# One core, graph network on Trainium2: in the message stage, both subtractions of the bfloat16 split on VectorE, and four of seven bins scaled by ScalarE

## The reference

```
for l in range(N_LAYERS):                      # 3
    f1 = relu(x[row] @ nb_W[l] + nb_b[l]);  f2 = relu(x[col] @ self_W[l] + self_b[l])
    h = relu(concatenate([f1, f2], axis=1) @ att1_W[l] + att1_b[l])
    mask = clip(sigmoid(h @ att2_W[l] + att2_b[l]) * (ZETA - GAMMA) + GAMMA, 0.0, 1.0)
    rowsum = segment_sum(mask, row, num_segments=n) + 1e-06
    d_inv_sqrt = clip(rowsum ** (-0.5), 0.0, 10.0)
    vals = mask * d_inv_sqrt[row] * d_inv_sqrt[col]
    x = segment_sum(vals[:, None] * x[col], row, num_segments=n)
    out = out + x
```

## Time and profile before

| | before |
|---|---|
| median of 3 runs | 4532.59 us (4524.75 to 4538.07) |
| the profiled execution | 4528.35 us, of which the span from first to last instruction is 4526.7 us |
| message stage, first layer | from the first scaling at 1960.68 us to the last `take` at 2422.54 us |
| message stages of all three layers | about 3 x 462 us, three tenths of the span |
| TensorE matmul, VectorE, GpSimd, ScalarE busy over the whole span | 87%, 82%, 56%, 43% |

### The profile page before, as it was taken

One profiled execution on the slowest core, in us unless ns is written; L12 is line 12 of the kernel. 1 busy time (PEld: TensorE's weight loads), 2 busy tenths in 40 slices (PEclk: granted clock), 3 DMA queues, 4 the chain that ended last, 5 costly groups with the idle time before them and its releaser, 6 DMA issues. The chain is left out here.

```text
span 4526.7 us, 258560 instructions
## 1 busy us (share of the span) xinstructions
PE 3923.0 (87%) x100368; PEld 3766.8 (83%) x100369; DVE 3699.7 (82%) x5871; ACT 1952.9 (43%) x4743; POOL 2522.8 (56%) x3439
## 2 busy tenths in 40 slices
PE   5888857888875999979997999979998899979997
PEld 5888857777774999968886999978887899979887
DVE  6666678988886888889996788889997788879998
ACT  4666636777762121135553111235554111125554
POOL 4555538978862222268885222248897222238987
PEclk7777769999997999989998999989999999989999
DMA  1000009999992777746662677746663677656665
GB/s 29 1 1 1 1 1 273 315 299 294 285 273 81 236 247 241 240 138 171 171 171 84 229 241 239 247 149 171 171 171 89 207 241 247 236 170 173 171 171 139
DMA packets 532058, 793.93 MB, mean 175 GB/s; under 512 B 66324, under 2 KB 466120, under 8 KB 531976
## 3 DMA queue, kind: packets, MB, share of 16 engines
q1 hardware_dynamic: 499048, 714.07, 49.5%
q0 software_dynamic: 32928, 78.72, 7.6%
HBM read 672.34 MB, written 120.24 MB: 175 GB/s over the span
## 5 line engine op out<-in xcount | busy, mean ns | idle before, releaser
L1330 POOL TENSOR_TENSOR message<-message 128x448 f32<-128x448 f32 x1029 | 1243.5, 1241 | 209.5 <-ACT message L1314 209.4
L1101 PE MATMUL pre_ps<-rows_a,hotT_a 128*128 128x64 bf16 x21609 | 1289.2, 193 | 52.1 <-DMA hotT_a<-hot_scratch 27.3
L1101 PE MATMUL pre_ps<-table,hotT_a 128*128 128x64 bf16 x21609 | 1288.7, 194 | 0.0
L1101 PEld LDWEIGHTS pre_ps<-rows_a,hotT_a 128*128 128x128 fp8e4 x21609 | 1131.3, 98 | 59.0 <-issue 58.8
L1101 PEld LDWEIGHTS pre_ps<-table,hotT_a 128*128 128x128 fp8e4 x21609 | 1131.8, 98 | 1.1 <-issue 1.0
L1341 DVE TENSOR_TENSOR message<-message 128x448 f32<-128x448 f32 x1029 | 994.2, 966 | 69.0 <-POOL message L1330 68.9
L1181 DVE SCALAR_TENSOR_TENSOR weighed<-pre_ps,w 128x448 f32<-128x448 f32 x1029 | 642.4, 624 | 309.5 <-PE pre_ps L1101 217.1
L1314 ACT ACTIVATE message<-high_ps,mask 128x64 f32<-128x64 f32 x3087 | 699.6, 326 | 298.4 <-PE high_ps L1273 279.2
L1285 PE MATMUL sum_ps<-message,hot_b 128*128 128x192 bf16 x7203 | 784.0, 247 | 7.4 <-DVE message L1341 5.7
L1273 PE MATMUL low_ps<-table,hot_b 128*128 128x64 bf16 x12348 | 528.7, 193 | 161.0 <-DMA hot_b<-hot_scratch 64.9
L1149 POOL TENSOR_SCALAR fresh<-gate 128x49 f32<-128x49 f32 x147 | 35.3, 240 | 1113.5 <-ACT gate L1129 1113.5
(11 more groups left out here) (149 smaller groups left out, 5130.0 us busy)
## 6 DMA issues: line engine op xcount, KB each, us to landing
hotT_a<-hot_scratch SPq DMA_DIRECT2D x1029, 224.0 KB, 4.6
hot_b<-hot_scratch SPq DMA_DIRECT2D x1029, 224.0 KB, 2.8
hot_scratch<-hot SPq DMA_DIRECT2D x343, 336.0 KB, 9.3
hot_a<-hot_scratch SPq DMA_DIRECT2D x147, 784.0 KB, 5.1
places<-slots_scratch POOLq DMA_DIRECT2D x686, 112.0 KB, 6.6
out<-res SPq DMA_DIRECT2D x1, 1536.0 KB
slots_scratch<-bins SPq DMA_DIRECT2D x49, 12.5 KB
raw<-in_src SPq DMA_DIRECT2D x1, 768.0 KB
```

Source lines behind the costliest of these rows:

```text
L1101: last = nc.tensor.matmul(pre_ps[g][:, j, :], hotT[:, b, g, end, j * P:(j + 1) * P].bitcast(FP8), table, start=end + part == 0, stop=end = ...
L1330: pool.tensor_tensor(message[:, g, :, 1, :], message[:, g, :, 0, :], top[:, g, :, 0, :, 1], ALU.subtract).then_inc(s["rest_ready"], 1)
```

## The change

LOW goes from 4 to 3: VectorE scales three bins out of PSUM (192 elements) and ScalarE four. The GpSimd block is removed; its subtraction becomes `rest` on VectorE, two groups late, and `third` goes from two groups late to three. VectorE's queue per group is then: scaling(q), rest(q-2), third(q-3), and `take` in the last group. At the end of the stage the left-over differences are written out.

```
-    LOW = min(4, G - 1)
+    LOW = min(3, G - 1)
...
-            @block.gpsimd
-            def _(pool):
-                def row(r, b, nth, first):
-                    for g in range(NG):
-                        q = r * NG + g
-                        pool.wait_ge(s["low_scaled"], q + 4)
-                        pool.wait_ge(s["high_scaled"], q + 4)
-                        pool.tensor_tensor(message[:, g, :, 1, :], message[:, g, :, 0, :], top[:, g, :, 0, :, 1],
-                                           ALU.subtract).then_inc(s["rest_ready"], 1)
-                each_row(pool, NB, row)
-
             @block.vector
             def _(dve):
...
+                def rest(q, r, g, b):
+                    dve.wait_ge(s["low_scaled"], q + 4)
+                    dve.wait_ge(s["high_scaled"], q + 4)
+                    dve.tensor_tensor(message[:, g, :, 1, :], message[:, g, :, 0, :], top[:, g, :, 0, :, 1],
+                                      ALU.subtract).then_inc(s["rest_ready"], 1)
...
-                        late(r, g, b, 2, first, third)
+                        late(r, g, b, 2, first, rest)
+                        late(r, g, b, 3, first, third)
                         if g == NG - 1 and not first:
                             take(r - 1, 1 - b)
                 each_row(dve, NB, row)
+                rest(Q - 2, NB - 1, NG - 2, 0)
+                third(Q - 3, NB - 1, NG - 3, 0)
+                rest(Q - 1, NB - 1, NG - 1, 0)
                 third(Q - 2, NB - 1, NG - 2, 0)
                 third(Q - 1, NB - 1, NG - 1, 0)
                 take(NB - 1, 0)
```

## The result

The changed kernel takes 4575.24 us in the median of four runs (4569.57 to 4582.81), the kernel before, with one more run beside them, 4535.33 us (4524.75 to 4542.38). The forecast was 4563 us, +30.

The account below looks back on a forecast made before the run. A loop through GpSimd and ScalarE was taken to set 9.395 us a row; VectorE's plain sum afterwards gives 9.58. Over 47 rows 8.7 us, plus 0.2 and 1.1 at the ends: 10.0 a layer, +30 for three, 4563 us (4542 to 4602).

Parts of the forecast that it names:

- What bounds the kernel now: Message stage: a row is a loop of GpSimd's seven instructions (8.63 us) plus 0.77 us waiting for ScalarE, 9.40 us.
- already full: VectorE in the message stage: its savings and the 0.53 us paid for each `rest` would nearly cancel.
- Steps 1 to 3: VectorE, message stage: `third` costs 0.53 us instead of 0.94, `rest` 0.53, scaling three bins 0.27 instead of 0.33.
- Steps 4 and 5: Message stage: ScalarE's four-bin scaling has 1.4 us to spare; TensorE's wait for the later `third` stays hidden.
- Step 5: TensorE finishes its gather 1.2 us after `third`, one turn (1.33 us) early; a sum four groups late loses that cover.
- Step 6: VectorE's queue: added semaphore waits of `rest`, 40 to 57 ns each, are worked off beside the running instruction.
- The stage with its ends: Message stage per layer: 8.7 us from 47 rows, +0.2 at the start, +1.1 at the end, together 10.0 us.
- Larger fixed cost: Rival, chance 0.04: VectorE instructions out of PSUM hold it longer; a row grows by 0.48 us, +71 us, near 4633.
- The stretch not GpSimd's: Rival, chance 0.02: both VectorE subtractions keep 0.94 us, 15.3 us a row, +870 us.
- Two subtractions overlapping: Rival, chance 0.05: `third` behind `rest` on VectorE hides the fixed 0.07 us; a row of 9.09 us, near 4494.
- Register work: Rival, chance 0.07: register and wait work in VectorE's queue shows, 0.84 us a row, +123 us, near 4686.

Follow-up runs that it names:

- e4_before_take5: The kernel before, with `take` in the sixth group of a row instead of the seventh: 4456.68 against 4528.82 us, ratio 0.9847.
- e2_pool_low3: The kernel before with LOW = 3 alone, both differences staying where they were: 4529.62 against 4528.82 us, ratio 1.0005.
- e1_low4: The changed kernel with LOW = 4 again, so only the difference is moved to VectorE: 4633.59 us against 4528.82 for the kernel before, ratio 1.0226.
- e7_late4: The changed kernel with LATE = 4 instead of 5 (sum four groups late): 4763.57 us against 4524.94 for the kernel before, ratio 1.0528.
- e3_low2: The changed kernel with LOW = 2, ScalarE scaling five of seven bins: 4495.08 us against 4528.82 for the kernel before, ratio 0.9929.
- e10_low21: The changed kernel with `take` one group earlier and VectorE scaling two bins or one in alternate groups: 4446.89 us against 4506.24 for the kernel before, ratio 0.9875.
- e5_spare_tt: The changed kernel plus an unused GpSimd subtraction of two SBUF tensors per group: 5528.84 us in one run, against 4524.94 for the kernel before.
- e6_spare_memset: The changed kernel plus an unused GpSimd memset of 448 elements per group: 4568.28 us in one run, against 4524.94 for the kernel before.
- e9_after_take5: The changed kernel with `take` in the sixth group of a row instead of the seventh: 4543.28 us against 4506.24 for the kernel before, ratio 1.0088.

## Why the prediction was right, and where it was off

- *What bounds the kernel now.* That a row was a loop through GpSimd with ScalarE's share was right (e4_before_take5). That VectorE was "already full" was wrong: 0.41 us of each stretched `third` were waiting in disguise, absorbing `take` (e4_before_take5) and the shorter scaling (e2_pool_low3) without a trace. The forecast didn't rest on it: it set a plain sum of VectorE's times for the row after beside the measured 9.395 us for the row before. Taken alone, the scaling of three bins was worth nothing in the kernel before; beside the moved difference it gave 0.46 us a row (e1_low4 against the changed kernel).
- *Steps 1 to 3.* The durations were right: 0.53, 0.53 and 0.27 us, and the order of instructions that no row had shown cost nothing more. The row is 9.61 us, not 9.58: the 0.53 is 0.533, fourteen times a row. 0.03 x 141 = 4 us.
- *Steps 4 and 5.* No wait for ScalarE, none for TensorE in the running rows. Step 5's cover was real, and it is gone with a sum four groups late, as the step says. But its 1.2 us for TensorE's part were too low: 1.66 in e7_late4.
- *Step 6.* No gap ahead of `rest` or `third`; the register work is hidden.
- *The stage with its ends.* +10.0 us were forecast for a layer's whole message stage. From the last split of the table before the stage (L1207) to the last `take` the three layers took 480.4 to 480.5 us before and 492.8, 492.8 and 493.9 after: +38 in all, against +30. Beside the 4 us of rounding, the tail is 4.24 us (4.31 in the second layer), not 4.07, and each layer lost 0.6 to 1.7 us in its first two rows. In the first layer TensorE stopped in the midst of a sum:

```profile
1985.38 0.67 PE L1285 MATMUL sum_ps<-message,hot_b 128*128 128x192 bf16 x6 [1.36 <-issue]
```

  and VectorE's next scaling and `rest` came late (10.24 us for that row instead of 9.61). The profile names nothing that TensorE waited for. The kernel before has such stops too, of 1.31 us near the start of its second and third stages, so they aren't the change's own; the cause wasn't tried.
- *The whole.* The two profiled executions differ by 4576.16 - 4528.35 = 47.8 us: 38 in the message stages, 6.5 before the first of them, 3.3 in the two later mask stages, which the change doesn't touch. By the medians it is 40 to 42 us, so of the 12 us above the forecast some 8 are the message stage's (row, ends) and the rest can't be told from differences between runs.
- *The rivals.* Larger fixed cost: refuted, `take` and the scaling at 0.27 and a row that e1_low4, e3_low2 and e10_low21 meet at four sizes of the scaling. The stretch not GpSimd's: refuted by e5_spare_tt and e6_spare_memset. Two subtractions overlapping: refuted, 0.53 and 0.54 in a row. Register work: not seen.

## What to carry to other kernels

When a stretched instruction on one engine goes with another engine's instructions, price the pair and not the single one: here GpSimd's subtraction and VectorE's exclude each other, 0.74 and 0.53 us, but the scaling, a VectorE instruction that reads PSUM, fits into GpSimd's time for nothing. Before moving work off a helper engine, look for what makes it idle: 0.77 and 1.12 us of idle time in alternate rows, behind a `take` that stood one group too late, were worth more than the whole move. And a VectorE that is never idle could be summed from starts to 0.2% here (five kernels, rows of 8.95 to 10.07 us): fill it until it meets the next engine, not to a round share of bins.

## What the runs showed of the hardware that I had not expected

In some runs VectorE's records grow with no change in its pace. In the changed kernel's first message stage a subtraction has a record of 0.61 us at the start and 0.76 at the end, always 0.53 from start to start. In e1_low4 the record goes from 0.62 to 1.18 us; two thirds into the stage it is 1.05:

```profile
2302.24 1.05 DVE L1336 TENSOR_TENSOR message<-message 128x448 f32<-128x448 f32 x1
2302.78 0.85 DVE L1351 TENSOR_TENSOR message<-low_ps,mask 128x256 f32<-128x256 f32 x1
```

Past the first rows VectorE is never idle in either stage, but that alone doesn't do it: in e9_after_take5 and e10_low21 it is never idle either, and the record still stands at 0.63 and 0.61 at the end. In e7_late4, with waits, it stays at 0.61 to 0.62. The end of the record seems to be the real one: the last `take`, which has to wait for the last sum, comes 1.07 us after the end of the last subtraction before and after the change alike, with records of 0.61, 0.76 and (second layer) 0.83. That explains 0.15 us of the longer tail, and the 4.31 us of the second layer's. Why the start runs ahead of the work, and only in some kernels, wasn't tried.
